# The last pass of an attention and FFN kernel: VectorE scales every chunk, GpSimd subtracts the rounding numbers

## The chip, the core and the metric

The kernel runs on one core of a Trainium2 chip. The metric is the device time of one execution in microseconds (us), as the median of several runs of the same program. The engines are PE (TensorE), DVE (VectorE), ACT (ScalarE), POOL (GpSimd) and SP (SyncE, which only issues transfers here). Each engine runs its own queue of instructions in order and waits for the others by semaphores.

## The reference

The input is x, 4096 rows of 256 numbers in float32. The first layer is attention with 16 heads of width 16, causal softmax in the one branch and a linear recurrence over the rows in the other, mixed by a learned gate, projected and added to x. The second layer, cut to its core, is what the change touches:

```python
x = x + attention(layernorm(x))
h = layernorm(x)
def quant_fp8(x):
    amax = jnp.max(jnp.abs(x))
    scale = jnp.minimum(448.0 / jnp.maximum(amax, 1e-12), 448.0)
    x_fp8 = jnp.clip(x * scale, -448.0, 448.0).astype(jnp.float8_e4m3fn)
    return x_fp8, 1.0 / scale
w_fp8, w_scale = quant_fp8(weight)            # 256 x 256
h_fp8, h_scale = quant_fp8(h)                 # 4096 x 256
out = (h_fp8.astype(f32) @ w_fp8.astype(f32).T * (h_scale * w_scale) + bias).astype(bf16)
return x + out.astype(f32)
```

The scale needs the largest absolute value of the whole of h, so nothing can be rounded before the last row is normalised.

## The kernel before, in words

The 4096 rows are cut into 8 chunks of 512 rows. The program has three parts, one after the other: a prologue (projections), the attention and the recurrence (most of the time), and the final part, in which everything that concerns this change stands.

The final part first merges the two branches chunk by chunk, normalises and finds the largest value; then one chain of tiny DVE instructions makes the scale (`small[:, 4:5]`, lines 1899 to 1904), and then the last pass runs over the 8 chunks. A chunk is a tile of 128 partitions by 1024 numbers. It is rounded to the 3 mantissa bits of fp8 without an fp8 type, in five steps:

1. `scl` = min(xn2 * scale, 448) (lines 1696 and 1910)
2. `magic` = the exponent bits of `scl` (line 1917, a bitwise and)
3. `magic` = max(magic, smallest normal) * 1.5 * 2^20 (line 1920)
4. `moved` = max(scl, -448) + magic, which drops the low bits (line 1923)
5. `r_bf` = moved - magic, the rounded number in bf16 (line 1928)

PE then turns `r_bf` (`turn_rounded`, line 1749), ACT copies it out of PSUM (line 1804), PE multiplies it by the rounded weights (`ffn`, line 1759), ACT adds bias and scale (line 1812), PE turns the result back (`turn_ffn`, line 1770), and DVE adds the residual `x1` and writes `o_f` (`add_ffn`, line 1935), which SP stores. PE's order in an iteration n is `turn_rounded(n)`, `turn_ffn(n-1)`, `ffn(n)`; DVE's is `quantise(n)`, `add_ffn(n-2)`. All buffers of the pass have two slots, for even and odd chunks.

Before the change DVE does step 1 for chunks 0 and 1 only. For chunks 2 to 7 POOL does it (`scale(n)`), as soon as step 4 of chunk n-2 has let go of the slot of `scl`; DVE takes up the tile by the semaphore `scaled_ahead`. Steps 2 to 5 are DVE's for all chunks. Nothing else runs on POOL in the last pass.

The order on each engine is the order in which the code is written; `pipeline` peels the first iterations and puts the others in a hardware loop. `free_sem(name, credit)` makes a semaphore that starts at the credit, so a wait for n+1 with a credit of 2 asks for chunk n-2.

Of the kernel before, what the change touches and what calls it, by code (L numbers as in the profile page):

```python
# [9 lines left out]
ALU = mybir.AluOpType  # L10
# [3 lines left out]
P = 128  # L14
# [3 lines left out]
NCH = T // CH  # L18
TPC = CH // P
# [24 lines left out]
FP8_MAX = 448.0  # L44
# [55 lines left out]
N_SCALE = 6  # L100
# [242 lines left out]
def preln_attention_ffn_kernel(nc, x, wqkv, bqkv, out_w, out_b, w_static, lam, gamma, gate_w1,  # L343
                               gate_b1, gate_w2, gate_b2, ffn_wt, ffn_b, out):
    ctx = ExitStack()
    with ctx:
        def sb(name, shape, dt=F32, where=ctx):
            return where.enter_context(nc.sbuf_tensor(name, shape, dt))

        def sem(name):  # L350
            return ctx.enter_context(nc.semaphore(name))
# [29 lines left out]
        neg_half = sb("neg_half", [P, TPC])  # L381

        weights_loaded, first_weights = sem("weights_loaded"), sem("first_weights")
        beats = sem("beats")
# [64 lines left out]
        stats2, mv2, rstd2, nmr2 = sem("stats2"), sem("mv2"), sem("rstd2"), sem("nmr2")  # L449
        xn2_made, amax_made, amax_all = sem("xn2_made"), sem("amax_made"), sem("amax_all")  # L450
        scale_chain, peak_ready = sem("scale_chain"), sem("peak_ready")
        scaled_ahead, trial_made = sem("scaled_ahead"), sem("trial_made")
        scaled, exponent_done, magic_done = sem("scaled"), sem("exponent_done"), sem("magic_done")
        shifted, rounded, r_turned = sem("shifted"), free_sem("rounded", 2), free_sem("r_turned", 2)
        rt_evac, ffn_ready = free_sem("rt_evac", 2), free_sem("ffn_ready", 2)
# [1123 lines left out]
        with fin:  # L1579
# [15 lines left out]
            nmr = sb("nmr2", [P, 2 * TPC], where=fin)  # L1595
            amax = sb("amax", [P, NCH], where=fin)
            small = sb("small", [P, 8], where=fin)
            trial = sb("trial", [P, TPC], where=fin)
            peaks = sb("peaks", [P, P], where=fin)
            scl = sb("scl", [P, 2, TPC * D], where=fin)  # L1600
            magic = sb("magic", [P, 2, TPC * D], where=fin)
# [9 lines left out]
            def tiles(it, par):  # L1611
                return bass.ds(it * (2 * TPC) + par * TPC, TPC)
# [4 lines left out]
            def pipeline(engine, *stages):  # L1617


                depth = max(lag for lag, _ in stages)  # L1620
                peeled = depth + depth % 2

                def step(it, par, whole):
                    for lag, stage in stages:
                        if whole or 0 <= it * 2 + par - lag < NCH:
                            stage(it + (par - lag) // 2, (par - lag) % 2)

                for k in range(peeled):
                    step(k // 2, k % 2, False)
                with engine.Fori(peeled // 2, NCH // 2) as it:  # L1630
                    step(it, 0, True)
                    step(it, 1, True)
                for k in range(NCH, NCH + depth):
                    step(k // 2, k % 2, False)

            with nc.Block() as block:
# [24 lines left out]
                @block.gpsimd  # L1661
                def _(pool):
                    def weigh(it, par):

                        pool.wait_ge(gate_chain, 3)
                        pool.wait_ge(diff_made, it * 2 + par + 3)
                        pool.tensor_tensor(diff[:, par].rearrange("p j (h v) -> p j h v", h=H),
                                           diff[:, par].rearrange("p j (h v) -> p j h v", h=H),
                                           alpha[:, tiles(it, par), :].unsqueeze(3).broadcast_to([P, TPC, H, HD]),
                                           ALU.mult).then_inc(diff_weighted, 1)  # L1670

                    def power(it, par):

                        pool.wait_ge(var2, it * 2 + par + 1)
                        own = slice(par * TPC, (par + 1) * TPC)
                        pool.tensor_tensor(rstd[:, own], var_eps[:, own], neg_half[:, :], ALU.pow).then_inc(rstd2, 1)
                        pool.wait_ge(rstd2, it * 2 + par + 1)
                        pool.tensor_tensor(nmr[:, own], neg_mean[:, own], rstd[:, own], ALU.mult).then_inc(nmr2, 1)

                    def residual(it, par):  # L1680

                        pool.wait_ge(x_again[par], it * 16 + 16)
                        pool.wait_ge(x1_made, it * 2 + par + 1)
                        pool.tensor_tensor(xb[:, par], xres[:, par],
                                           outb_sb[:, :].unsqueeze(1).broadcast_to([P, TPC, D]), ALU.add)\
                            .then_inc(xb_made, 1)

                    pipeline(pool, (1, residual), (0, weigh), (2, power))

                    pool.tensor_scalar(trial[:, :], neg_half[:, :], neg_half[:, 0:1], FP8_MAX, ALU.mult, ALU.min)\  # L1690
                        .then_inc(trial_made, 1)

                    def scale(n):

                        pool.wait_ge(shifted, n - 1)
                        pool.tensor_scalar(scl[:, n % 2], xn2[:, n * TPC:(n + 1) * TPC, :].rearrange("p j n -> p (j n)"),  # L1696
                                           small[:, 4:5], FP8_MAX, ALU.mult, ALU.min).then_inc(scaled_ahead, 1)

                    pool.wait_ge(scale_chain, N_SCALE)
                    for n in range(2, NCH):  # L1700
                        scale(n)

                @block.tensor
                def _(pe):
# [115 lines left out]
                def _(dve):  # L1820
# [85 lines left out]
                    def quantise(it, par):  # L1906
                        n1 = it * 2 + par + 1

                        if isinstance(it, int):
                            dve.tensor_scalar(scl[:, par], xn2[:, tiles(it, par), :].rearrange("p j n -> p (j n)"),  # L1910
                                              small[:, 4:5], FP8_MAX, ALU.mult, ALU.min).then_inc(scaled, 1)
                            dve.wait_ge(scaled, n1)
                        else:
                            dve.wait_ge(scaled_ahead, n1 - 2)
                            dve.sem_inc(beats, 1)

                        dve.tensor_scalar(magic[:, par].bitcast(I32), scl[:, par].bitcast(I32), EXPONENT_BITS, None,  # L1917
                                          ALU.bitwise_and).then_inc(exponent_done, 1)
                        dve.wait_ge(exponent_done, n1)
                        dve.tensor_scalar(magic[:, par], magic[:, par], FP8_MIN_NORMAL, ROUND_TO_3_BITS, ALU.max,  # L1920
                                          ALU.mult).then_inc(magic_done, 1)
                        dve.wait_ge(magic_done, n1)
                        dve.scalar_tensor_tensor(out=moved[:, par], in0=scl[:, par], scalar=-FP8_MAX, in1=magic[:, par],  # L1923
                                                 op0=ALU.max, op1=ALU.add).then_inc(shifted, 1)
                        dve.wait_ge(shifted, n1)

                        dve.wait_ge(r_turned, n1)
                        dve.tensor_tensor(r_bf[:, par].rearrange("p j n -> p (j n)"), moved[:, par], magic[:, par],  # L1928
                                          ALU.subtract).then_inc(rounded, 1)

                    def add_ffn(it, par):

                        dve.wait_ge(ffn_turned, it * 2 + par + 3)
# [2 lines left out]
                                          PS[:, 6 + par, :].bitcast(BF16).rearrange("p (j n) -> p j n", n=D), ALU.add)\  # L1936
                            .then_inc(out_made, 1)

                    pipeline(dve, (0, quantise), (2, add_ffn))


# [35 lines left out]
```

## Time and profile before

| | |
|---|---|
| median of 3 runs | 1748.61 us (1747.91 to 1751.28) |
| the profiled execution's own time | 1747.87 us |
| its span, first to last instruction | 1746.1 us |
| busy share of the span: PE, DVE, ACT, POOL | 93%, 87%, 80%, 72% |
| mean granted TensorE clock | 0.961 of full speed |
| step 1 of chunk 0 starts | 1696.52 us |
| last `add_ffn` starts | 1741.41 us |

The shares of the whole span describe the attention part. The last pass is the stretch from 1696.5 us to the end, under 3% of the span, and its limit is read from its own rows. In a timeline row the first number is the start, the second the time that the instruction or the merged group took, both in us; the bracket is the idle time of the engine before it and what ended it.

### The profile page before, as it was taken

The page shows a single profiled execution, that of the slowest core. Times are in us where ns is not written, and L with a number is a line of the kernel's source. Part 1 is how long each engine was busy: PE and PEld are TensorE (multiplying, and loading weights), DVE is VectorE, ACT ScalarE, POOL GpSimd, SP SyncE. Part 2 cuts the span into 40 slices and gives each one's busy share as a digit, 9 for nine tenths or more (in the row PEclk, how much of TensorE's full clock was granted, in tenths as well). Part 3 has the DMA queues.
Part 4 walks back from the last instruction along what each step waited for, and adds up shares of the span by engine and source line. Part 5 has one row for each costly group of instructions (what it writes and reads, how often), then busy time and mean ns, then how long its engine had stood idle before and what let it go on. Part 6 is the DMA issues. An engine that isn't in the chain of part 4 may idle for free. (4 is left out here: it accounts for less than half of the span.)

```text
span 1746.1 us, 44612 instructions
## 1 busy us (share of the span) xinstructions
PE 1615.5 (93%) x17578; PEld 581.9 (33%) x17582; DVE 1521.4 (87%) x1736; ACT 1388.5 (80%) x2835; POOL 1249.6 (72%) x1159
## 2 busy tenths in 40 slices
PE   6995799999999999999999999999999999999655
PEld 3541133323333332233333323333333232333542
DVE  6679899999899999998999999989999999930688
ACT  4651488998988889989878899898888889898234
POOL 3525587778777778787777777877788888870545
PEclk9995699999999999999999999999999999999786
DMA  5885423141222332412224223221242221200612
GB/s 164 276 278 157 96 64 97 54 117 54 78 75 75 88 86 75 100 58 77 65 78 113 76 71 81 78 75 61 78 118 81 82 80 47 81 5 14 244 48 97
DMA packets 115347, 163.23 MB, mean 93 GB/s; under 512 B 30080, under 2 KB 57792, under 8 KB 115136
## 3 DMA queue, kind: packets, MB, share of 16 engines
q1 hardware_dynamic: 112608, 158.74, 31.0%
q8 instruction: 137, 2.24, 0.6%
q10 hardware_dynamic: 2528, 1.64, 0.3%
q14 instruction: 74, 0.61, 0.1%
HBM read 121.87 MB, written 38.01 MB: 92 GB/s over the span
## 5 line engine op out<-in xcount | busy, mean ns | idle before, releaser
L1528 DVE TENSOR_REDUCE pmax<-PS 128x2 f32<-128x1024 f32 (+2 forms) x1120 | 1203.9, 1130 | 84.1 <-PE PS L1327 66.4
L1481 ACT ACTIVATE probs<-PS 128x512 f32<-128x512 f32 (+3 forms) x2304 | 1149.6, 576 | 155.5 <-PE PS L1365 76.5
L1392 PE MATMUL PS<-probs,V_g 128*17 128x256 f32 (+3 forms) x5064 | 395.8, 385 | 4.1 <-ACT o_t L1502 3.7
L1235 POOL TENSOR_TENSOR v_exp<-v_exp,k_rows 128x512 f32<-128x512 f32 x256 | 321.8, 1284 | 27.0 <-DMA v_exp<-qkv_t 26.5
L1365 PE MATMUL PS<-Q_st,K_st 50*128 50x512 f16 (+3 forms) x1408 | 288.7, 364 | 7.9 <-ACT probs L1481 6.5
L1277 POOL TENSOR_TENSOR state<-odd,q_rows 128x514 f32<-128x514 f32 x256 | 281.7, 1132 | 6.1
L1327 PE MATMUL PS<-K_st,Q_st 48*128 48x512 f16 (+3 forms) x1408 | 272.2, 357 | 0.2
L1392 PE MATMUL PS<-probs,V_first 128*17 128x256 f32 (+2 forms) x3296 | 264.9, 393 | 2.2 <-ACT o_t L1502 2.2
L1365 PE MATMUL PS<-Q_st,K_first 50*128 50x512 f16 (+3 forms) x896 | 193.6, 378 | 12.1 <-ACT probs L1481 6.1
L1327 PE MATMUL PS<-K_first,Q_st 48*128 48x512 f16 (+1 forms) x832 | 178.8, 391 | 19.6 <-DVE pmax L1528 19.4
L1266 POOL COPY carry<-odd 128x4 f32<-128x4 f32 x64 | 12.0, 187 | 253.9 <-DVE odd L1563 253.9
L1365 PEld LDWEIGHTS PS<-Q_st,K_st 50*128 50x128 f16 x1408 | 80.3, 93 | 295.3 <-ACT probs L1481 241.7
L1245 POOL TENSOR_TENSOR pairs<-pairs,v_exp 128x512 f32<-128x512 f32 x128 | 162.7, 1291 | 0.1
L1392 PEld LDWEIGHTS PS<-probs,V_g 128*17 128x17 f32 x5064 | 84.0, 95 | 184.7 <-issue 110.4
L1490 ACT ACTIVATE pairs<-v_exp,decay 128x256 f32<-128x256 f32 x256 | 128.7, 544 | 9.8 <-POOL v_exp L1235 9.8
L1365 PEld LDWEIGHTS PS<-Q_st,K_first 50*128 50x128 f16 x896 | 51.8, 93 | 209.0 <-ACT probs L1481 159.1
L1392 PEld LDWEIGHTS PS<-probs,V_first 128*17 128x17 f32 x3296 | 54.7, 95 | 143.9 <-issue 89.6
L1271 POOL TENSOR_TENSOR odd<-odd,pairs 128x512 f32<-128x512 f32 x64 | 96.5, 1508 | 5.0
L1563 DVE TENSOR_TENSOR_SCAN odd<-decay_x,sums 128x516 f32<-128x516 f32 x64 | 83.1, 1298 | 11.0 <-POOL sums L1256 11.0
L1256 POOL TENSOR_TENSOR sums<-sums,pairs 128x512 f32<-128x512 f32 x64 | 82.8, 1294 | 5.0
L725 PE MATMUL PS<-xn_t,w_parts 128*128 128x512 f16 x336 | 79.2, 389 | 4.5 <-DVE xn_t L902 4.3
L1425 PE MATMUL PS<-state,sum_e 128*32 128x256 f32 x1024 | 77.8, 394 | 0.0
(194 smaller groups left out, 1494.9 us busy)
## 6 DMA issues: line engine op xcount, KB each, us to landing
v_exp<-qkv_t SPq DMA_DIRECT2D x256, 256.0 KB
qkv_t<-proj SPq DMA_DIRECT2D x24, 512.0 KB, 4.1
qk_parts<-parts SPq DMA_DIRECT2D x16, 512.0 KB, 5.1
Q_st<-qk_parts SPq DMA_DIRECT2D x192, 32.0 KB, 3.6
v_rows<-vaug SPq DMA_DIRECT2D x8, 544.0 KB, 6.1
xin<-x SPq DMA_DIRECT2D x8, 512.0 KB, 6.8
k_rows<-qkv_t SPq DMA_DIRECT2D x16, 256.0 KB, 4.0
q_rows<-qkv_t SPq DMA_DIRECT2D x16, 256.0 KB, 6.1
```

The lines of the kernel that those rows point to most:

```text
L1235: pool.tensor_tensor(v_exp[:, n % RING], v_exp[:, n % RING], k_rows[:, b % 2], ALU.mult)\
L1245: pool.tensor_tensor(pairs[:, B % 2, k:k + 2], pairs[:, B % 2, k:k + 2], v_exp[:, slot:slot + 2, 1:CH:2], ALU.add).then_inc(pair_made, 1)
L1256: pool.tensor_tensor(own[:, :, 1:], own[:, :, 1:], pairs[:, B % 2, :, 1:PAIR:2], ALU.add)\
L1271: pool.tensor_tensor(middle, middle, pairs[:, B % 2, :, 0:PAIR:2], ALU.add).then_inc(middle_made, 1)
L1277: pool.tensor_tensor(state[:, B % STATES, k].rearrange("p (c e) -> p c e", e=PLACES), own[:, k, 0:PAIR + 1].unsqueeze(2).broadcast_to([P, ...
L1327: mm = pe.matmul(PS[:, bank, 0:width], Q_st[rows, c, pair, j * P:(j + 1) * P], keys[rows, pair, blk * CH:blk * CH + width], start=True, st ...
L1365: mm = pe.matmul(PS[:, bank, 0:CH - r * P], keys[rows, pair, kt * P:(kt + 1) * P], Q_st[rows, c, pair, r * P:CH], start=True, stop=(kt < T ...
L1392: mm = pe.matmul(PS[h * VW:h * VW + VN, out_bank(g, s), first:end], v[:, kt, h * VN:(h + 1) * VN], probs[:, tile % P_SLOTS, h, first - r * ...
L1481: act.activation(probs[:, tile % P_SLOTS, h, 0:CH - r * P], PS[:, step[5], 0:CH - r * P], ACT.Exp, scale=SCORE_SCALE).then_inc(exp_done, 1)
L1490: act.activation(pairs[:, B % 2, s % BATCH, :], v_exp[:, s % RING, 0:CH:2], ACT.Identity, scale=decay[:, 0, col:col + 1]).then_inc(u_scale ...
L1528: dve.tensor_reduce(pmax[:, s % 2, pair * TPC + j:GH * TPC:PAIRS * TPC, blk], PS[:, bank:bank + SIDES, 0:width], AX.X, ALU.max).then_inc(m ...
L1563: dve.tensor_tensor_scan(odd[:, s % 2].rearrange("p u (x e) -> p (u x) e", e=2)[:, :, 0], decay_x[:, s % (HALF * SWEEP_BATCHES), :], sums[ ...
```

## The change

DVE does step 1 for all chunks, in front of steps 2 to 4. Step 5 goes from DVE to POOL, as `difference(n)`, which waits for step 4 of its chunk (`shifted`) and for PE to have read the slot of `r_bf` (`r_turned`). Step 2 of chunk n now waits for step 5 of chunk n-2 (`rounded`), since it overwrites `magic`. The semaphores `scaled_ahead` and `trial_made`, the small instruction on the tile `trial`, and the hardware loop of DVE in the last pass go; DVE's instructions there are written out. Code that follows moves up by some lines: step 1 is line 1904 after, step 2 line 1909, step 3 line 1912, step 4 line 1915, step 5 line 1692 and `add_ffn` line 1921.

```diff
-                    pool.tensor_scalar(trial[:, :], neg_half[:, :], neg_half[:, 0:1], FP8_MAX, ALU.mult, ALU.min)\
-                        .then_inc(trial_made, 1)
-
-                    def scale(n):
-
-                        pool.wait_ge(shifted, n - 1)
-                        pool.tensor_scalar(scl[:, n % 2], xn2[:, n * TPC:(n + 1) * TPC, :].rearrange("p j n -> p (j n)"),
-                                           small[:, 4:5], FP8_MAX, ALU.mult, ALU.min).then_inc(scaled_ahead, 1)
-
-                    pool.wait_ge(scale_chain, N_SCALE)
-                    for n in range(2, NCH):
-                        scale(n)
+                    def difference(n):
+
+                        pool.wait_ge(shifted, n + 1)
+                        pool.wait_ge(r_turned, n + 1)
+                        pool.tensor_tensor(r_bf[:, n % 2].rearrange("p j n -> p (j n)"), moved[:, n % 2], magic[:, n % 2],
+                                           ALU.subtract).then_inc(rounded, 1)
+
+                    for n in range(NCH):
+                        difference(n)
...
                     def quantise(it, par):
                         n1 = it * 2 + par + 1
 
-                        if isinstance(it, int):
-                            dve.tensor_scalar(scl[:, par], xn2[:, tiles(it, par), :].rearrange("p j n -> p (j n)"),
-                                              small[:, 4:5], FP8_MAX, ALU.mult, ALU.min).then_inc(scaled, 1)
-                            dve.wait_ge(scaled, n1)
-                        else:
-                            dve.wait_ge(scaled_ahead, n1 - 2)
-                            dve.sem_inc(beats, 1)
+                        dve.tensor_scalar(scl[:, par], xn2[:, tiles(it, par), :].rearrange("p j n -> p (j n)"),
+                                          small[:, 4:5], FP8_MAX, ALU.mult, ALU.min).then_inc(scaled, 1)
+                        dve.wait_ge(scaled, n1)
+                        dve.wait_ge(rounded, n1)
...
-                        dve.wait_ge(shifted, n1)
-
-                        dve.wait_ge(r_turned, n1)
-                        dve.tensor_tensor(r_bf[:, par].rearrange("p j n -> p (j n)"), moved[:, par], magic[:, par],
-                                          ALU.subtract).then_inc(rounded, 1)
-
...
-                    pipeline(dve, (0, quantise), (2, add_ffn))
+                    for n in range(NCH + 2):
+                        if n < NCH:
+                            quantise(n // 2, n % 2)
+                        if n >= 2:
+                            add_ffn((n - 2) // 2, n % 2)
```

DVE's instructions of one chunk in the steady part of the pass, before (the body of the hardware loop, even chunk; `ISA` and `REGISTER_ALU` rows are register work):

```order
L1917 TENSOR_SCALAR magic<-scl 128x1024 [waits scaled_ahead]
L1919 REGISTER_ALU
L1920 TENSOR_SCALAR magic<-magic 128x1024 [waits exponent_done]
L1923 SCALAR_TENSOR_TENSOR moved<-scl,magic 128x1024 [waits magic_done]
L1928 TENSOR_TENSOR r_bf<-moved,magic 128x1024 [waits r_turned,shifted]
```

The same place on DVE after:

```order
L1904 TENSOR_SCALAR scl<-xn,small 128x1024
L1909 TENSOR_SCALAR magic<-scl 128x1024 [waits rounded,scaled]
L1912 TENSOR_SCALAR magic<-magic 128x1024 [waits exponent_done]
L1915 SCALAR_TENSOR_TENSOR moved<-scl,magic 128x1024 [waits magic_done]
L1921 TENSOR_TENSOR o_f<-x,PS 128x1024 [waits out_stored0,ffn_turned]
```

The subtraction has gone from the end of the chunk and the scaling has come in at its front; `add_ffn` of the chunk two back now stands right behind step 4.

POOL from the end of the merging to the end of the program, before:

```order
L1676 TENSOR_TENSOR rstd<-var_eps,neg_half 128x4 [waits var2]
L1678 TENSOR_TENSOR nmr<-neg_mean,rstd 128x4 [waits rstd2]
L1690 TENSOR_SCALAR trial<-neg_half 128x4
L1696 TENSOR_SCALAR scl<-xn,small 128x1024 [waits shifted,scale_chain]
L1696 TENSOR_SCALAR scl<-xn,small 128x1024 [waits shifted] x5
```

and after:

```order
L1674 TENSOR_TENSOR rstd<-var_eps,neg_half 128x4 [waits var2]
L1676 TENSOR_TENSOR nmr<-neg_mean,rstd 128x4 [waits rstd2]
L1692 TENSOR_TENSOR r_bf<-moved,magic 128x1024 [waits r_turned,shifted] x8
```

Six instructions with one tile as input have become eight with two, and each now starts when DVE has finished step 4 of the same chunk.

## Rows read from the trace of the kernel before

**Rows 1.** Pass and tail: length, busy PE PEld DVE ACT POOL, PEclk, DMA.
```profile
1696.50:1736.25 39.75, 22.34 (x129) 12.00 (x132) 38.83 (x40) 16.62 (x21) 28.45 (x6) 0.60 0.18 67
1736.25:1742.65 6.40, 2.67 (x27) 1.66 (x28) 3.55 (x3) 3.14 (x4) 0.00 (x0) 0.95 0.44 164
```

**Rows 2.** Timeline of one chunk in the steady part, DVE and POOL.
```profile
1722.33 0.68 DVE L1917 TENSOR_SCALAR magic<-scl 128x1024 int32<-128x1024 int32 x1
...
1723.78 1.23 DVE L1923 SCALAR_TENSOR_TENSOR moved<-scl,magic 128x1024 f32<-128x1024 f32 x1
...
1725.04 1.23 DVE L1928 TENSOR_TENSOR r_bf<-moved,magic 128x1024 bf16<-128x1024 f32 x1
...
1725.10 4.73 POOL L1696 TENSOR_SCALAR scl<-xn,small 128x1024 f32<-128x1024 f32 x1 [0.25 <-DVE moved L1923]
...
1726.18 1.22 DVE L1935 TENSOR_TENSOR o_f<-x,PS 128x1024 f32<-128x1024 bf16 x1
...
1727.31 0.69 DVE L1917 TENSOR_SCALAR magic<-scl 128x1024 int32<-128x1024 int32 x1
```

**Rows 3.** Timeline of the first chunk and the start of the second.
```profile
1696.52 0.75 DVE L1910 TENSOR_SCALAR scl<-xn,small 128x1024 f32<-128x1024 f32 x1
...
1698.77 1.23 DVE L1923 SCALAR_TENSOR_TENSOR moved<-scl,magic 128x1024 f32<-128x1024 f32 x1
...
1700.16 4.96 POOL L1696 TENSOR_SCALAR scl<-xn,small 128x1024 f32<-128x1024 f32 x1 [9.35 <-DVE moved L1923]
1701.17 1.61 DVE L1910 TENSOR_SCALAR scl<-xn,small 128x1024 f32<-128x1024 f32 x1
```

**Rows 4.** Instruction groups of POOL, by form: busy, mean ns, idle before.
```profile
L1271 POOL TENSOR_TENSOR odd<-odd,pairs 128x512 f32<-128x512 f32 x64 | 96.5, 1508 | 5.0
L1256 POOL TENSOR_TENSOR sums<-sums,pairs 128x512 f32<-128x512 f32 x64 | 82.8, 1294 | 5.0
...
L1696 POOL TENSOR_SCALAR scl<-xn,small 128x1024 f32<-128x1024 f32 x6 | 28.4, 4744 | 10.6 <-DVE moved L1923 10.6
L1684 POOL TENSOR_TENSOR xb<-xres,outb_sb 128x1024 f32<-128x1024 f32 x8 | 18.9, 2368 | 0.5 <-issue 0.5
L1667 POOL TENSOR_TENSOR diff<-diff,alpha 128x1024 f32<-128x1024 f32 x8 | 15.5, 1932 | 61.3 <-DVE diff L1833 61.3
```

**Rows 5.** One instruction group of DVE, in the same columns.
```profile
L1851 DVE TENSOR_TENSOR x<-PS,xb 128x1024 f32<-128x1024 f32 x4 | 4.9, 1219 | 4.5 <-PE PS L1732 4.5
```

**Rows 6.** Timeline of the prologue, a small DVE instruction behind POOL.
```profile
58.21 4.07 POOL L606 TENSOR_TENSOR parts<-proj,parts 128x2048 f16<-128x2048 f32 x1 [5.37 <-DVE parts L896]
...
61.20 1.10 DVE L880 TENSOR_SCALAR var_eps<-mv 128x4 f32<-128x4 f32 x1
```

**Rows 7.** Durations of L880 in ns, minimum, median and maximum.
```profile
L880 DVE TENSOR_SCALAR var_eps<-mv x8: 170/172/1103, 9.4 to 100.1; 128x4 f32<-128x4 f32 x8
```

**Rows 8.** Durations of L1563, in the same columns.
```profile
L1563 DVE TENSOR_TENSOR_SCAN odd<-decay_x,sums x64: 1210/1223/2274, 191.0 to 1558.1; 128x516 f32<-128x516 f32 x64
```

**Rows 9.** Timeline of the attention part, a DVE scan between two POOL products.
```profile
1101.72 1.27 POOL L1235 TENSOR_TENSOR v_exp<-v_exp,k_rows 128x512 f32<-128x512 f32 x1 [1.79 <-DMA v_exp<-qkv_t]
1102.06 2.02 DVE L1563 TENSOR_TENSOR_SCAN odd<-decay_x,sums 128x516 f32<-128x516 f32 x1
1103.20 1.95 POOL L1235 TENSOR_TENSOR v_exp<-v_exp,k_rows 128x512 f32<-128x512 f32 x1 [0.21 <-DMA v_exp<-qkv_t]
```

**Rows 10.** Timeline of the tail, behind the last subtraction.
```profile
1735.00 1.23 DVE L1928 TENSOR_TENSOR r_bf<-moved,magic 128x1024 bf16<-128x1024 f32 x1
...
1736.36 0.62 PE L1749 MATMUL PS<-ident_bf,r_bf 128*128 128x128 bf16 x8 [0.93 <-DVE r_bf L1928]
...
1738.40 0.81 PE L1759 MATMUL PS<-r_t,wq 128*128 128x512 bf16 x3 [0.80 <-ACT r_t L1804]
```

**Rows 11.** Timeline of the steady part, PE's products and turns.
```profile
1718.64 1.49 PE L1759 MATMUL PS<-r_t,wq 128*128 128x512 bf16 x3 [1.15 <-ACT r_t L1804]
...
1731.38 1.03 PE L1749 MATMUL PS<-ident_bf,r_bf 128*128 128x128 bf16 x8 [1.46 <-DVE r_bf L1928]
```

More of the change, by code:

```diff
@@ L451, in preln_attention_ffn_kernel @@
         scale_chain, peak_ready = sem("scale_chain"), sem("peak_ready")
-        scaled_ahead, trial_made = sem("scaled_ahead"), sem("trial_made")
         scaled, exponent_done, magic_done = sem("scaled"), sem("exponent_done"), sem("magic_done")
@@ L1597, in preln_attention_ffn_kernel @@
             small = sb("small", [P, 8], where=fin)
-            trial = sb("trial", [P, TPC], where=fin)
             peaks = sb("peaks", [P, P], where=fin)
```

## Prediction, made before the changed kernel ran

> **What bounds the kernel now.** I read the busy time by stretches first, because the shares over the whole span describe the attention and say nothing of the last pass. Two stretches matter [rows 1]. From 1696.50 to 1736.25 us DVE is busy 38.83 of 39.75 us, so DVE is the bound there, with PE at 22.34 and ACT at 16.62. POOL shows 28.45 us and is not the bound: it waits 0.25 us for DVE before a scaling [rows 2]. Behind the last subtraction there is a chain through all engines, 6.40 us, and then the last store.
>
> The timeline of one chunk shows how DVE's time is made up [rows 2]. From step 2 of one chunk (1722.33) to step 2 of the next (1727.31) are 4.98 us: steps 2 and 3 take 1.45 us up to the start of step 4, and the further starts lie 1.26, 1.14 and 1.13 us apart, with no waiting. An instruction that needs its predecessor's result starts 0.03 to 0.04 us behind its end, one that does not about 0.09 us ahead of it. POOL's scaling starts 0.09 us behind the end of step 4 (1725.01 to 1725.10) and takes 4.73 us, inside the 4.98.
>
> **The part on DVE alone.** The change takes 1.23 us of subtraction from DVE and gives it 0.75 us of scaling [rows 3]. The scaling of the next chunk needs nothing from the instruction in front of it, so the steps of a chunk become 0.79 (scale to step 2), 0.73, 0.73, 1.26 less 0.12 because `add_ffn` need not wait for step 4, and 1.13. That is 4.52 us, 0.46 us less than now, for the chunks that have an `add_ffn`. If nothing else happened this would be a gain of some 3 us. The instructions that go with the loop and the 4-number instruction on `trial` are worth nothing: DVE's register work between chunks hid in the 1.22 us of the instruction before it, and `trial` ran on an idle POOL. Their cost without that cover would be tenths of a microsecond.
>
> **What the subtraction costs on POOL.** The trace has no subtraction of two float32 tiles into bf16 on POOL. The nearest row is an addition of 1024 numbers with two float32 inputs, 2368 ns. From both sides: the multiplication by a repeated alpha takes 1932 ns; the plain addition of 512 numbers 1294 ns, or 2588 for twice the size with its start counted twice; the one that reads every second number 1508 ns, or 3016 [rows 4]. I take 2.37 us, the same size and kind of inputs, and keep 1.93 and 3.02 for the range.
>
> The Trainium skill (GPSIMD Engine Reference, Performance versus the Vector engine) gives 4497 ns for such an addition of 2048 numbers, from which an estimate of 2.25 us for 1024 follows; the eight chunks would then come out 1 us shorter than in my sum. The same page (Engine selection) calls an operation with one input on GpSimd roughly line-rate and one with two inputs about twice as slow. The trace disagrees on the first half: one input took 4744 ns here, two inputs 2368 [rows 4].
>
> **What the subtraction does to DVE.** This is the term that decides. Line 880 is a DVE operation of 4 numbers, one tile from SBUF, that takes 170 ns at the median and once 1103 [rows 7]. In that case it started at 61.20 and ended at 62.30, while POOL's two-input instruction ran from 58.21 to 62.28 [rows 6]: it ended 0.02 us after POOL did. The scan of line 1563, with two SBUF inputs, takes 1.22 us at the median and up to 2.27 [rows 8]. In the attention part one starts at 1102.06 beside a POOL product that ends at 1102.99, and ends at 1104.08, which is 1.09 us after POOL's end. The next POOL product starts at 1103.20, inside the scan, and takes 1.95 instead of 1.27 us: it ends 1.07 us after the scan [rows 9]. So a POOL instruction with two inputs and a DVE instruction of one of these two kinds exclude each other for their whole length. The later one shows its start and finishes, after the other's end, in its own time less about 0.13 us. Operations of DVE with one operand in PSUM, like `add_ffn`, are not of these kinds: the addition that takes `xb` took 1219 ns at the mean [rows 5] in a stretch in which POOL worked through its own additions of 2368 ns.
>
> The Trainium skill says this as contention, without a size (GPSIMD Engine Reference, Key points): GpSimd shares its SBUF interfaces with VectorE and contends with instructions in a two-port mode or with two SBUF inputs. By that rule all of steps 1 to 4 are in conflict with the subtraction, and `add_ffn` is not; the trace agrees, and adds that the wait lasts the whole instruction.
>
> Now one chunk after the change, t being the end of step 4 of chunk n. POOL starts its subtraction at t + 0.09, as the scaling that waits for the same semaphore does now [rows 2], and ends at t + 2.46. DVE does `add_ffn` of chunk n-2 until t + 1.14; then its scaling of chunk n+1 stands waiting, and ends at 2.46 + 0.75 - 0.13 = t + 3.08. Steps 2 and 3 take 0.73 each with their gaps, step 4 1.27. The sum is 5.81 us per chunk against 4.98. Behind the waiting scaling are queued steps 2 to 4 of that chunk and the next `add_ffn`, so the whole pass waits with it.
>
> Chunks 0 and 1 have no `add_ffn` behind them. There the scaling of the next chunk starts 0.08 us ahead of step 4's end and has the port before POOL asks for it. POOL comes in behind it, at t + 0.67, ends 2.24 later at t + 2.91, and step 2 ends at 2.91 + 0.56 = t + 3.47; with 0.73 and 1.27 the chunk takes 5.47 us.
>
> **The sum.** Step 4 of chunk 0 ends at 1700.00 in both kernels (1698.77 + 1.23) [rows 3]. Then come two chunks of 5.47 and five of 5.81: 1700.00 + 10.94 + 29.05 = 1739.99. The last subtraction ends 2.46 later, at 1742.45, against 1736.23 now (1735.00 + 1.23) [rows 10]. That is 6.2 us later.
>
> The tail stays the same chain: turns, copy, products, bias, turns, `add_ffn`, store. PE is not late inside the pass: `turn_ffn(n-2)` stands behind `turn_rounded(n-1)`, which ends 1.03 us after POOL's subtraction [rows 11], and its own turns take about as long, so it is done at t(n-1) + 4.6, and DVE asks for it at t(n-1) + 5.8. The new wait of step 2 for the subtraction of two chunks back costs nothing: that ended a whole chunk earlier. The tail's PE work ran at a granted clock of 0.95, the pass at 0.60 [rows 1]. If the tail after the change should run at the lower of the two levels (1.2 instead of 2.4 GHz), the two sets of turns cost 1.03 each instead of 0.62 and three products 1.49 instead of 0.81 [rows 10, 11], 1.5 us in all. I leave that out of the sum and in the range.
>
> The profiled execution took 1747.87 us and would take 1754.1; its span goes from 1746.1 to 1752.3. The median shown lies 0.74 us above that execution, so the forecast for the median is 1748.6 + 6.2 = 1754.8 us.
>
> **The rivals.**
> A, no conflict: every instruction keeps its own time. For it speaks that steps 2 to 5 ran mostly at full speed beside POOL's scaling, at 0.68 and 1.23 us [rows 2]; against it the rows of lines 880 and 1563 [rows 6, 9], in which POOL has two inputs as it will have. Chunks take 3.44 us without `add_ffn` and 4.56 with it. The first `add_ffn` waits some 2 us for its chain, which is an estimated 8.9 us long from step 4 of chunk 0: 2.46 for the subtraction, the 5.2 that lie between 1736.23 and the last `add_ffn` at 1741.41, and 1.2 for the lower clock. The last step 4 ends at 1708.9 + 1.1 + 3.4 + 4 x 4.56 = 1731.7, the last subtraction at 1734.2: 2.0 us earlier, 1746.6 us. A gain over 0.2% needs still more.
> B, the conflict behaves as with the scaling now: DVE loses only once per chunk. The scaling of chunk 1 took 1.61 instead of 0.75 [rows 3], 0.86 us. With that, seven chunks take 7 x 0.86 = 6.0 us more than in A, less the 2 us that A waits for its first `add_ffn` anyway: 1746.6 + 4.0 = 1750.6 us, no change by the measure below. Against it, again, [rows 6, 9]. It decides if POOL gives the port back within its instruction.
> C, POOL is also kept out by `add_ffn`, and waits for it before it begins. Then a chunk takes 5.81 + 1.13 us, and the time is 1754.8 + 5 x 1.13 = 1760.5. Against it stands the pair of 1219 and 2368 ns [rows 4, 5], neither of which shows a wait of that size.
>
> **How the numbers follow.** What a measurement of this kernel can tell from no change is about 0.2%, 3.5 us. The chances are 0.77 for the forecast, 0.05 for A, 0.12 for B and 0.06 for C. The forecast's own ends are those of the subtraction: eight times 1.93 gives 1754.8 - 3.5 = 1751.3, eight times 2.59 gives 1756.6, and eight times 3.02 gives 1760.0, which I hold for unlikely since its row skips every second number. With the tail's clock 1756.3. The range is 1750.4 to 1758.0, which takes in B. Slower over 0.2% is above 1752.1: nearly all of the forecast and C, 0.79. Within: B, A and a little of the forecast, 0.19. Faster 0.02.
>
> **What would show it.** In the profile after, the scaling on DVE (line 1904) should take about 2.0 us in chunks 3 to 7 and end 0.6 us after POOL's subtraction; step 2 (line 1909) should take about 2.8 us in chunks 1 and 2. POOL should show 8 subtractions of 2.4 us, step 4's starts should be 5.8 us apart, and `add_ffn` should stay at 1.2 us. A scaling of 0.75 us beside a running subtraction would prove me wrong, and a POOL instruction stretched by `add_ffn` would show C. A waiting `add_ffn` would mean that PE's chain has become the bound.

## The result and the profile after

The changed kernel takes 1754.55 us (median of 11 runs, 1752.71 to 1759.35), the kernel before on the same chips 1748.95 us (11 runs, 1747.20 to 1751.89). The ratio is 1.0035, with a 95% interval of 1.0026 to 1.0043: slower by 4.5 to 7.5 us. The forecast was 1754.8 us and slower. Among all the runs reported below, two (2133.46 us with ScalarE scaling, 7567.31 us of the kernel before) lie far outside the others and are left out of the ratios.

The stretches of the changed kernel, with the columns of [rows 1]: from the first scaling to the end of the last subtraction, and from there to the end of the last `add_ffn`.

```profile
1696.88:1742.06 45.18, 23.17 (x129) 12.80 (x132) 43.05 (x38) 17.25 (x21) 19.66 (x8) 0.54 0.16 60
1742.06:1749.35 7.29, 3.63 (x27) 2.50 (x28) 2.44 (x2) 2.50 (x4) 0.00 (x0) 0.73 0.36 136
```

Before, the first of these stretches ran from 1696.52 to 1736.23, 39.71 us [rows 3, 10]; now it is 45.18. DVE shows as busy for 43.05 us of it, with 38 instructions where there were 40. Busy here means started and not ended: the wait for the other engine lies inside the instruction, and no idle time in front of anything tells of it. As in the prediction, "the port" below is what POOL and these DVE instructions keep each other from; the runs show that they exclude each other, not what it is that they share. The list of waits gives DVE none but the two of the tail. This is why the durations have to be compared form by form.

One chunk of the steady part of the changed kernel, DVE and POOL in one timeline, answers to [rows 2]:

```profile
1715.62 1.23 DVE L1915 SCALAR_TENSOR_TENSOR moved<-scl,magic 128x1024 f32<-128x1024 f32 x1
1716.76 1.21 DVE L1921 TENSOR_TENSOR o_f<-x,PS 128x1024 f32<-128x1024 f32 x1
1716.92 2.35 POOL L1692 TENSOR_TENSOR r_bf<-moved,magic 128x1024 bf16<-128x1024 f32 x1 [3.34 <-DVE moved L1915]
1717.89 1.93 DVE L1904 TENSOR_SCALAR scl<-xn,small 128x1024 f32<-128x1024 f32 x1
1719.86 0.69 DVE L1909 TENSOR_SCALAR magic<-scl 128x1024 int32<-128x1024 int32 x1
1720.59 0.69 DVE L1912 TENSOR_SCALAR magic<-magic 128x1024 f32<-128x1024 f32 x1
1721.32 1.23 DVE L1915 SCALAR_TENSOR_TENSOR moved<-scl,magic 128x1024 f32<-128x1024 f32 x1
```

POOL starts 0.07 us behind step 4's end (1716.85 to 1716.92) and ends at 1719.27. `add_ffn` beside it takes its usual 1.21 us. The scaling takes 1.93 instead of 0.75 us and ends at 1719.82, 0.55 us behind POOL. It takes 1.93 us in each of chunks 3 to 7. From step 4 to step 4 are 5.70 us.

The start of chunk 1, where no `add_ffn` stands in between, answers to [rows 3]:

```profile
1699.13 1.22 DVE L1915 SCALAR_TENSOR_TENSOR moved<-scl,magic 128x1024 f32<-128x1024 f32 x1
1700.27 0.75 DVE L1904 TENSOR_SCALAR scl<-xn,small 128x1024 f32<-128x1024 f32 x1
1700.43 2.78 POOL L1692 TENSOR_TENSOR r_bf<-moved,magic 128x1024 bf16<-128x1024 f32 x1 [9.54 <-DVE moved L1915]
1701.05 2.71 DVE L1909 TENSOR_SCALAR magic<-scl 128x1024 int32<-128x1024 int32 x1
```

Here both engines wait, one after the other: POOL's 2.78 us contain 0.43 us for the scaling in front of it, and step 2 takes 2.71 instead of 0.69 and ends at 1703.76, again 0.55 us behind POOL's end at 1703.21.

### The profile page after: what moved, and what is told of

Same layout as the page of the kernel before. It is cut to its first block and busy times, and to the rows that moved or that the text cites. A ratio compares the mean times of both kernels' runs of the same rounds, so it can differ in the third digit from the quotient of the medians.

```text
span 1752.8 us, 44584 instructions
## 1 busy us (share of the span) xinstructions
PE 1617.6 (92%) x17578; PEld 583.2 (33%) x17582; DVE 1524.2 (87%) x1734; ACT 1388.2 (79%) x2835; POOL 1241.9 (71%) x1160
```

## The experiments

Each edit is shown against the changed kernel, with `...` where lines are left out. Times compare with the kernel before on the same chip: its median was 1747.10 us beside the first four experiments, 1748.52 beside the two versions in the other order on ScalarE, and 1748.24 beside the others. Where one run is given, its total says little, because what precedes the pass varies: the pass starts at 1697.93 us in the profile with 8 columns and at 1694.30 in the one with half. There the rows of the pass carry the argument. "The pass" is the time from the first scaling's start (on ScalarE, where that scales chunk 0) to the last subtraction's end: 39.7 us before, 45.2 after the change. "Distance" is from step 4's start to the next in the steady part: 4.98 and 5.70.

### GpSimd subtracts 8 columns

```diff
+                    pool.memset(r_bf[:, :, :, :].rearrange("p a j n -> p (a j n)"), 0.0).then_inc(gate_exp, 1)
+                    pool.wait_ge(gate_exp, 2)
...
-                        pool.tensor_tensor(r_bf[:, n % 2].rearrange("p j n -> p (j n)"), moved[:, n % 2], magic[:, n % 2],
+                        pool.tensor_tensor(r_bf[:, n % 2].rearrange("p j n -> p (j n)")[:, 0:8],
+                                           moved[:, n % 2, 0:8], magic[:, n % 2, 0:8],
```

> As the changed kernel, but GpSimd subtracts only 8 of the 1024 numbers of a row in each chunk; the other columns of r_bf hold zeros, so the layer's product is left out for them. Every wait and every instruction stays. Theory (a GpSimd subtraction and a VectorE instruction that uses two SBUF reads exclude each other for their whole length): with next to no subtraction the scaling on VectorE takes 0.75 to 0.8 us in all chunks, step 2 0.69, and starts of step 4 lie 4.5 to 4.6 us apart in the steady part instead of 5.70; from the start of step 1 to the end of the last subtraction about 35.5 us instead of 45.2, so some 1744 to 1746 us. Rival (the new waits between the two engines, rounded and shifted, cost the time, or the loop written out does): the distance stays at 5.2 us or more although GpSimd does next to nothing.

Measured: one run at 1744.70 us. The timeline of the same place, DVE and POOL:

```profile
1716.80 1.23 DVE L1918 SCALAR_TENSOR_TENSOR moved<-scl,magic 128x1024 f32<-128x1024 f32 x1
1717.94 1.22 DVE L1924 TENSOR_TENSOR o_f<-x,PS 128x1024 f32<-128x1024 f32 x1
1718.10 0.20 POOL L1694 TENSOR_TENSOR r_bf<-moved,magic 128x8 bf16<-128x8 f32 x1 [4.31 <-DVE moved L1918]
1719.07 0.75 DVE L1907 TENSOR_SCALAR scl<-xn,small 128x1024 f32<-128x1024 f32 x1
1719.85 0.69 DVE L1912 TENSOR_SCALAR magic<-scl 128x1024 int32<-128x1024 int32 x1
```

The scaling is back at 0.75 us and the distance is 4.51. All waits, the order and the loop written out are as in the changed kernel, so none of them costs the time; the length of the subtraction does. The pass took 33.9 us, less than the 35.5 expected, and one `add_ffn` in it waited 0.74 us for PE.

### GpSimd subtracts half

```diff
...
-                        pool.tensor_tensor(r_bf[:, n % 2].rearrange("p j n -> p (j n)"), moved[:, n % 2], magic[:, n % 2],
+                        pool.tensor_tensor(r_bf[:, n % 2].rearrange("p j n -> p (j n)")[:, 0:512],
+                                           moved[:, n % 2, 0:512], magic[:, n % 2, 0:512],
```

> As the changed kernel, but GpSimd subtracts 512 of the 1024 numbers; the other half of r_bf holds zeros. Theory (exclusion by whole instructions): the subtraction takes 1.27 us, from 0.07 to 1.34 us behind the end of step 4, of which add_ffn covers 1.06; the scaling behind it takes about 0.9 us, since a wait of 0.28 us overlaps with its own start by 0.13 to 0.2 us. Step 4's starts lie 4.6 to 4.7 us apart. Rival (both engines share the bandwidth of the memory, and VectorE loses in proportion to what GpSimd moves): half of the 1.18 us that the scaling loses now, so a scaling of 1.3 us and a distance of 5.1 us.

Measured, one run at 1742.45 us:

```profile
1711.10 1.27 POOL L1694 TENSOR_TENSOR r_bf<-moved,magic 128x512 bf16<-128x512 f32 x1 [3.34 <-DVE moved L1918]
1712.07 0.85 DVE L1907 TENSOR_SCALAR scl<-xn,small 128x1024 f32<-128x1024 f32 x1
```

The subtraction ends at 1712.37 and the scaling at 1712.92, 0.55 us behind. Half of the work costs DVE 0.10 us per chunk, the whole of it 1.18. That is no sharing of bandwidth, which would have made it 0.59, and the distance is 4.62 us, not 5.1. What counts is how far the POOL instruction reaches beyond `add_ffn`, here from 1712.15 to 1712.37. The pass took 36.5 us, 2.6 more than with 8 columns; that this run's total is nevertheless 2.3 us shorter comes from what lies around the pass, a start 3.6 us earlier and a tail of 5.18 us instead of 6.44.

### A copy of one tile in place of the subtraction

```diff
-                        pool.tensor_tensor(r_bf[:, n % 2].rearrange("p j n -> p (j n)"), moved[:, n % 2], magic[:, n % 2],
-                                           ALU.subtract).then_inc(rounded, 1)
+                        pool.tensor_copy(r_bf[:, n % 2].rearrange("p j n -> p (j n)"), moved[:, n % 2])\
+                            .then_inc(rounded, 1)
```

> As the changed kernel, but GpSimd's subtraction of two tiles is a copy of one tile (moved into r_bf, float32 to bf16), so the magic numbers are not taken away. Theory as told by the rows of the kernel before (two inputs on GpSimd exclude, one input mostly does not): the copy may take 1 to 5 us, the scaling stays at 0.75 to 1.6 us and does not end right behind the copy. Rival (any GpSimd instruction of this size excludes VectorE for its whole length): the scaling of chunks 3 to 7 ends 0.5 to 0.6 us behind the copy's end, and step 4's distance is 3.4 us plus the copy's time, if that is over 1.1 us.

Measured, one run at 1744.93 us. First a chunk without `add_ffn`, then, behind the dots, one with it:

```profile
1700.15 0.75 DVE L1904 TENSOR_SCALAR scl<-xn,small 128x1024 f32<-128x1024 f32 x1
1700.30 1.49 POOL L1692 CAST r_bf<-moved 128x1024 bf16<-128x1024 f32 x1 [9.53 <-DVE moved L1915]
1700.93 1.41 DVE L1909 TENSOR_SCALAR magic<-scl 128x1024 int32<-128x1024 int32 x1
...
1717.75 1.04 POOL L1692 CAST r_bf<-moved 128x1024 bf16<-128x1024 f32 x1 [3.47 <-DVE moved L1915]
1718.73 0.75 DVE L1904 TENSOR_SCALAR scl<-xn,small 128x1024 f32<-128x1024 f32 x1
```

Without `add_ffn`, step 2 ends 0.55 us behind the copy (1702.34 and 1701.79), as behind a subtraction. So my reading that one input on GpSimd does not exclude was wrong, and the rival is right for a copy; for the old scaling form, below, it is not. With `add_ffn` there is nothing to see, because a copy of 1.04 us fits under it. The rival's sum for the distance, meant for a copy of over 1.1 us, was not put to the test.

### All on VectorE

```diff
-                    for n in range(NCH):
-                        difference(n)
...
+                        dve.wait_ge(shifted, n1)
+                        dve.wait_ge(r_turned, n1)
+                        dve.tensor_tensor(r_bf[:, par].rearrange("p j n -> p (j n)"), moved[:, par], magic[:, par],
+                                          ALU.subtract).then_inc(rounded, 1)
```

> All five steps on VectorE, GpSimd idle in the last pass. Theory (the change gained nothing since the subtraction's 2.35 us stand in VectorE's way except for the 1.06 us beside add_ffn, which is as much as VectorE's own subtraction of 1.23 us takes): step 4's starts lie 5.73 to 5.78 us apart against 5.70 in the changed kernel, 4.65 without add_ffn against 5.40, and the last subtraction ends 1.27 us behind step 4 instead of 2.42. From the start of step 1 to the end of the last subtraction 42.6 us, 2.6 less than the changed kernel's 45.2 and 2.9 more than the 39.7 before: about 1751.8 us. Rival (GpSimd did take work off VectorE, and the loss comes from elsewhere): this kernel is slower than the changed one by about 8 times 0.5 to 1.2 us, 1758 to 1764 us.

Measured: 1752.25 us, ratio to the kernel before 1.0030 (1.0018 to 1.0041). The distance is 5.77 us, 4.64 without `add_ffn`, and the pass 42.9 us:

```profile
1715.95 0.75 DVE L1894 TENSOR_SCALAR scl<-xn,small 128x1024 f32<-128x1024 f32 x1
...
1719.44 1.22 DVE L1908 TENSOR_TENSOR r_bf<-moved,magic 128x1024 bf16<-128x1024 f32 x1
1720.59 1.21 DVE L1915 TENSOR_TENSOR o_f<-x,PS 128x1024 f32<-128x1024 f32 x1
1721.72 0.74 DVE L1894 TENSOR_SCALAR scl<-xn,small 128x1024 f32<-128x1024 f32 x1
```

So GpSimd's subtraction relieved VectorE of next to nothing: with it the distance is 5.70, without GpSimd 5.77. This pass is 2.3 us shorter than the changed kernel's, mostly in the first chunks (4.64 us instead of 5.40) and at the end, where the last subtraction takes 1.22 us instead of 2.35. The ratios (1.0030 and 1.0035) have intervals that overlap and do not show that gain. The tail, from the last subtraction's end to the start of the last `add_ffn`, is 6.45 us in this profile, 6.07 in the changed kernel's and 5.18 before.

### ScalarE scales, GpSimd subtracts

ScalarE gets the scaling of all chunks, two ahead, and DVE keeps steps 2 to 4 and `add_ffn`.

```diff
-                    pipeline(act, (0, rounded_columns), (0, dequantise))
+                    def scale(it, par):
+
+                        if not isinstance(it, int) or it > 0:
+                            act.wait_ge(shifted, it * 2 + par - 1)
+                        act.activation(scl[:, par], xn2[:, tiles(it, par), :].rearrange("p j n -> p (j n)"), ACT.Identity,
+                                       scale=small[:, 4:5]).then_inc(scaled, 1)
+
+                    pipeline(act, (0, scale), (2, rounded_columns), (2, dequantise))
...
-                        dve.tensor_scalar(scl[:, par], xn2[:, tiles(it, par), :].rearrange("p j n -> p (j n)"),
-                                          small[:, 4:5], FP8_MAX, ALU.mult, ALU.min).then_inc(scaled, 1)
```

> As the changed kernel, but ScalarE scales every chunk (without the min, which step 4's rounding makes superfluous), two chunks ahead; VectorE has steps 2 to 4 and add_ffn, GpSimd the whole subtraction. VectorE's own work is 3.8 us per chunk. Theory (exclusion by whole instructions): step 2 of the next chunk stands behind the subtraction, and ends at t + 2.42 + 0.55, so step 4's starts lie 4.96 us apart, as far as before the change although VectorE has 1.2 us less to do than then; 4.8 in the chunks without add_ffn. From the start of the pass to the end of the last subtraction 40.6 us against 39.7 before: about 1 us slower than the kernel before. Rival (the loss in the changed kernel is special to the scaling's pointer operand, or to its place right behind the subtraction's start): 3.8 to 4.1 us apart, about 1742 us.

Measured: 1750.12 us, ratio 1.0011 (1.0001 to 1.0021), a distance of 4.97 to 5.03 us (4.61 without `add_ffn`, 4.8 expected) and a pass of 40.5 us. DVE has one instruction less per chunk than in the changed kernel, and another of its instructions takes the wait, step 3 in the first chunk shown here. Behind it stands a later chunk:

```profile
1700.09 2.72 POOL L1692 TENSOR_TENSOR r_bf<-moved,magic 128x1024 bf16<-128x1024 f32 x1 [10.00 <-DVE moved L1920]
...
1700.64 2.72 DVE L1917 TENSOR_SCALAR magic<-magic 128x1024 f32<-128x1024 f32 x1
...
1719.26 2.36 POOL L1692 TENSOR_TENSOR r_bf<-moved,magic 128x1024 bf16<-128x1024 f32 x1 [2.62 <-DVE moved L1920]
...
1720.34 1.22 DVE L1926 TENSOR_TENSOR o_f<-x,PS 128x1024 f32<-128x1024 f32 x1 [1.16 <-PE PS L1765]
...
1721.48 0.69 DVE L1914 TENSOR_SCALAR magic<-scl 128x1024 int32<-128x1024 int32 x1
```

Step 3 has no pointer operand and ends at 1703.36, 0.55 us behind POOL: the effect belongs neither to the scaling nor to its operand. In the steady part the chain over PE and ACT was late too. In the later chunk shown, and in the next one, no DVE instruction is stretched: `add_ffn` waits 1.16 and 1.22 us for PE, and the distance is 4.98 and 5.03 all the same. So the exclusion is shown by the first chunks, and that the steady distance came out at the expected 4.96 is partly luck.

### ScalarE scales, VectorE does the rest

The same edit on ACT, with the subtraction on DVE as in the version all on VectorE.

> As the kernel before, but ScalarE scales every chunk and GpSimd is idle in the pass; VectorE has steps 2 to 5 and add_ffn. Theory: 4.98 us per chunk with add_ffn as before; 3.85 without it against 5.49 and 4.56 before, since VectorE neither scales chunk 1 nor is held up by GpSimd; from the start of the pass to the last subtraction's end 37.7 us against 39.7 before, so about 2 us faster than before. Rival (ScalarE's scaling of about 1.1 us comes late, behind its waits for TensorE in the same queue): 5.2 us or more per chunk and slower than before.

Measured: 1746.69 us, ratio 0.9989 (0.9979 to 0.9998), a distance of 4.98 us, 3.85 without `add_ffn`, and a pass of 37.8 us. As expected.

### The subtraction split

ACT scales chunks 1 to 7, DVE chunk 0. In chunks 2 to 6 DVE subtracts columns 512 to 1023 and POOL columns 0 to 511 (in `difference`); in the other chunks DVE subtracts all.

```diff
-                        difference(n)
+                        if 2 <= n < NCH - 1:
+                            difference(n)
+                        else:
+                            pool.wait_ge(r_turned, n + 2)
+                            pool.sem_inc(rounded, 1)
...
+                        low = 512 if 2 <= n1 - 1 < NCH - 1 else 0
+                        dve.tensor_tensor(r_bf[:, par].rearrange("p j n -> p (j n)")[:, low:TPC * D],
+                                          moved[:, par, low:TPC * D], magic[:, par, low:TPC * D],
+                                          ALU.subtract).then_inc(rounded_high, 1)
```

> A version meant to beat both: ScalarE scales chunks 1 to 7, VectorE chunk 0; in chunks 2 to 6 GpSimd subtracts 512 columns and VectorE the other 512, in chunks 0, 1 and 7 VectorE subtracts all. Theory: VectorE's half takes 0.69 us right behind step 4, then GpSimd's half (1.27 us) runs under add_ffn (1.21 us), which needs no second SBUF read. 4.5 to 4.6 us per chunk against 4.98 before. From the start of the pass to the last subtraction's end 35.3 us against 39.7: 4 us faster than before, about 1743 to 1744 us. Rival (GpSimd gets the port first and VectorE's half waits for it, or the chain over TensorE and ScalarE becomes the bound): 5.0 us or more apart and no gain.

Measured: 1747.58 us, ratio 0.9994 (0.9985 to 1.0003), so nothing of the 4 us expected. The distances were 4.47, 5.45, 5.30, 5.03 and 4.46 us. Its list of waits from 1711 to 1722 us (us in total, times, longest) says why:

```profile
ACT ffn_t L1814 <- PE PS L1761: 5.9, 3, 2.0
...
DVE o_f L1947 <- PE PS L1772: 1.7, 2, 0.9
```

`add_ffn` waits for the turned result, and ACT waits 2.0 us for the products in every chunk. ACT's row of scaling 1.14, copy 1.02, wait 1.98 and bias 1.45 us is longer than DVE's. That was the rival's second half; its first half, that GpSimd takes the port first, did not occur.

### The subtraction split, other order on ScalarE

```diff
-                    pipeline(act, (0, scale), (2, rounded_columns), (2, dequantise))
+                    pipeline(act, (2, rounded_columns), (0, scale), (2, dequantise))
```

> As the split version, but ScalarE's scaling of a chunk two ahead stands between its copy of the turned tile and its bias step, where it waited 1.98 us for the products, instead of in front of the copy. Theory (the split version fell short because ScalarE's row of scaling 1.14, copy 1.02, wait 1.98 and bias 1.45 us takes 5.4 us per chunk, longer than VectorE's 4.5): the scaling now lies inside that wait, the row is 4.5 us, step 4's starts lie 4.5 to 4.7 us apart, and the time is 1743 to 1745 us when the kernel before takes 1748. Rival (TensorE at its lower clock, or the turns, bound the chain): still 5.0 us or more apart, and no change against the split version.

Measured: 1742.62 us, ratio 0.9966 (0.9952 to 0.9980): 3.5 to 8.4 us faster than the kernel before, and so faster than the changed kernel too. The distance is 4.45 us and the pass 34.7:

```profile
1716.41 0.69 DVE L1939 TENSOR_TENSOR r_bf<-moved,magic 128x512 bf16<-128x512 f32 x1
1716.45 1.77 POOL L1693 TENSOR_TENSOR r_bf<-moved,magic 128x512 bf16<-128x512 f32 x1 [2.67 <-DVE moved L1934]
1716.80 1.45 ACT L1814 ACTIVATE ffn_t<-PS,ffnb_sb,small 128x512 bf16<-128x512 f32 x2
1717.02 1.22 DVE L1947 TENSOR_TENSOR o_f<-x,PS 128x1024 f32<-128x1024 f32 x1
1718.15 0.69 DVE L1928 TENSOR_SCALAR magic<-scl 128x1024 int32<-128x1024 int32 x1
```

DVE's half holds the port first, so POOL's half shows 1.77 instead of 1.27 us and ends at 1718.22. It lies under `add_ffn`, and step 2 keeps its 0.69 us.

### ScalarE scales, VectorE does the rest, other order on ScalarE

The same change of order in the version without GpSimd.

> As the version with ScalarE scaling and VectorE doing all the rest, with the same other order on ScalarE. Theory: VectorE sets 4.98 us per chunk as it did there, so only the end can gain: the tail from the last subtraction's end to the last add_ffn, 5.7 us there, becomes 5.2 as in the kernel before; 1746 us when the kernel before takes 1748, and some 2 us behind the split version in this order. Rival (nothing but the noise of a microsecond separates the two): both within 0.7 us of each other.

Measured: 1747.16 us, ratio 0.9991 (0.9982 to 0.9999), a distance of 4.98, a pass of 37.8 and a tail of 5.1 us. Against the same version in the first order (ratio 0.9989) nothing is left to see. The split version in this order is 4.5 us ahead by the medians, more than the 2 expected. Its pass is 3.1 us shorter: 2.7 from five distances of 4.45 instead of 4.98, which is what the half on GpSimd under `add_ffn` gives, and 0.5 because VectorE scales chunk 0 itself there, in 0.75 us instead of ScalarE's 1.15. Its tail was 0.9 us longer in the profiles (6.00 and 5.10). So the half on GpSimd is worth nearly the 3 us that the prediction's sum without a conflict hoped for from the whole; what else is in the 4.5 us the rows do not show.

### The old scaling form in the place of the subtraction

```diff
-                        pool.tensor_tensor(r_bf[:, n % 2].rearrange("p j n -> p (j n)"), moved[:, n % 2], magic[:, n % 2],
-                                           ALU.subtract).then_inc(rounded, 1)
+                        pool.tensor_scalar(r_bf[:, n % 2].rearrange("p j n -> p (j n)"), moved[:, n % 2],
+                                           small[:, 4:5], FP8_MAX, ALU.mult, ALU.min).then_inc(rounded, 1)
```

> As the changed kernel, but GpSimd's instruction is the form that it had before the change, a tensor_scalar with a pointer operand, mult and min, here from moved to r_bf (the magic numbers are not taken away). The copy of one tile took 1.04 us and held up VectorE like the subtraction. If the scaling before the change took 4.7 us because VectorE kept the port from it nearly all the time, it takes 1.0 to 1.3 us here under add_ffn, and step 4's starts lie 4.5 us apart. If the form itself takes 4 us or more and keeps the port, the next scaling ends 0.55 us behind it and the distance is 7 us or more. If it takes 4 us or more and leaves the port free for most of it, the distance stays at 4.5 to 5.3 us.

Measured: one run at 1755.51 us. The form takes 3701 to 4137 ns on POOL, but DVE's instructions beside it are not held up in this chunk:

```profile
1715.68 4.05 POOL L1692 TENSOR_SCALAR r_bf<-moved,small 128x1024 bf16<-128x1024 f32 x1 [3.56 <-DVE moved L1915]
1716.63 0.75 DVE L1904 TENSOR_SCALAR scl<-xn,small 128x1024 f32<-128x1024 f32 x1
1717.42 0.69 DVE L1909 TENSOR_SCALAR magic<-scl 128x1024 int32<-128x1024 int32 x1
...
1720.19 3.70 POOL L1692 TENSOR_SCALAR r_bf<-moved,small 128x1024 bf16<-128x1024 f32 x1 [0.46 <-DVE moved L1915]
1721.78 1.22 DVE L1921 TENSOR_TENSOR o_f<-x,PS 128x1024 f32<-128x1024 f32 x1 [1.68 <-PE PS L1765]
1722.91 1.52 DVE L1904 TENSOR_SCALAR scl<-xn,small 128x1024 f32<-128x1024 f32 x1
```

In the next chunk the scaling does wait, and ends 0.54 us behind POOL (1724.43 and 1723.89). The distances are 4.5 in some chunks and 6.7 to 7.3 in others, most of the difference being `add_ffn` waiting for PE. POOL's last instruction took 3.70 us, from 1738.48 to 1742.18, although DVE did nothing from 1739.51 on. So the form is long by itself, and in the chunk shown first it left the port free for DVE's three one-tile instructions. The first of the three cases did not occur. The second's sign, a scaling that ends about 0.55 us behind, and the third's distance each hold in some chunks only. Why the form is so long and which part of it holds the port stays open.

## Why the prediction was right

**The scaling that waits for the whole subtraction** was the term that decided, and it is shown: 1.93 us where 2.0 was forecast, 0.55 us behind POOL's end where 0.62 was. The chunk came out at 5.70 instead of 5.81 us, without `add_ffn` at 5.40 instead of 5.47. Of the 0.11 us too much, 0.07 came from the 0.13 us that I took off the waiting scaling for its start (0.20 was right; for step 2 it is 0.14), and 0.02 each from POOL's start and its duration. The 8 columns show that nothing else in the change costs the time, and the half that the price follows the reach of the POOL instruction and not the bytes.

**The subtraction's duration**, 2.37 us by the nearest row, measured 2.35 [rows 4].

**The gain on VectorE alone**, 0.46 us per chunk, is real where the cover holds: 4.51 us with the 8 columns, 4.52 forecast. It was lost inside the wait.

**The tail** was taken as unchanged, and was not: 6.07 us from the subtraction's end to the last `add_ffn` against 5.18. Its first turns took 1.03 us, those at the end 0.62, and the granted clock of the tail is 0.73 where it was 0.95 [rows 1]. I had priced the lower level at 1.5 us and left it out of the sum. The rows of the tail:

```profile
1742.18 1.03 PE L1744 MATMUL PS<-ident_bf,r_bf 128*128 128x128 bf16 x8 [1.58 <-POOL r_bf L1692]
...
1744.81 1.12 PE L1754 MATMUL PS<-r_t,wq 128*128 128x512 bf16 x3 [0.74 <-ACT r_t L1799]
...
1747.47 0.62 PE L1765 MATMUL PS<-ident_bf,ffn_t 128*128 128x128 bf16 x8 [1.54 <-ACT ffn_t L1807]
```

So the clock rose within the tail: granted were 0.50 from 1742.1 to 1744.1 and 0.93 from 1746.0 on, and the tail grew by 0.89 us and not by the whole 1.5. Whether the change causes the lower clock there is open: with half of the subtraction the granted clock of the tail was 0.94 and the tail 5.18 us, with 8 columns 0.72 and 6.44.

The profile's own sum is 0.37 (the pass starts later) + 5.47 + 0.89 = 6.7 us of span, against 6.2 forecast: the pass was forecast 0.75 us too long, start and tail 1.26 too short. The medians differ by 5.6 us. The mechanism was right, but that the forecast hit the median within 0.3 us is luck: errors of about 1 us cancelled, and the changed kernel's own times spread over 6.6 us.

**Rival A** (no conflict) is refuted by the 1.93 us, and **B** (one loss of 0.86 us as beside the scaling) by that and by the 5.40 us per chunk without `add_ffn`, where B gives 3.44 + 0.86 = 4.30; the experiment with the old form shows that B's rows came from an instruction that can leave the port free for much of its time. **C** (`add_ffn` excludes POOL too) is refuted by POOL's unstretched 2.35 us, which begins 0.16 us behind the start of `add_ffn`, and by the 1.21 us of `add_ffn`.

**Where my reasons were thinner than they looked:** I put the exclusion down to two inputs on GpSimd. The copy with one input excludes as well. I also took 4744 ns as the price of one input; the copy took 1040 ns, so that price belongs to the form with a pointer operand, mult and min.

## What to carry to other kernels

Work moved from VectorE to GpSimd frees VectorE only as far as it lies under VectorE instructions that do not exclude it, here one with an operand in PSUM; cut it to that size and leave the rest. Such a wait shows in no list of waits: compare an instruction's duration with its own minimum, and its end with the other engine's. Before trusting an engine to be free, add up its row including its own waits: ScalarE's scaling put inside its wait for the products cost nothing (4.45 us from step 4 to step 4), and in front of it made single chunks up to 1.0 us longer (5.45).

## What the runs showed of the hardware

- A VectorE instruction of the one-tile form (0.69 to 0.75 us for 1024 numbers a partition) that starts while a GpSimd subtraction or copy still has some time to run (0.30 us or more) ends 0.55 us behind it, whether it is the scaling, step 2 or step 3. Of those on two SBUF tiles only the scan of the attention part was seen to wait; it ended 1.09 us behind [rows 9]. Step 4 never met a subtraction.
- GpSimd waits in the same way: 2.78 for 2.35 us behind the scaling, 1.49 for 1.04 us likewise, and 1.77 for 1.27 us behind VectorE's half of the subtraction.
- The addition with one operand in PSUM took 1.21 or 1.22 us beside any of these. No run tells whether that comes from the PSUM operand or from its having only one tile in SBUF.
- On GpSimd 1024 float32 numbers in each of 128 partitions took 1.04 us for a copy to bf16, 2.35 for a subtraction of two tiles, and 3.7 to 4.1 for one tile with a pointer scalar, mult and min.
- ScalarE took 1.14 us to scale the same tile and did not disturb VectorE.
